# The first tile's queries and keys of each attention, projected into the score banks before the last products of the stage ahead

## What is computed

```python
x = x + band_attention(layernorm(x), ctx, ctx)       # |i - j| <= 128
x = x + ffn(layernorm(x), ...)                        # two layers of:
    h = shift_token(x)                                # half of the columns from the row before
    q, k, v = split(h @ wqkv)                         # 8 heads of 64
    q = l2norm(q) * qs;  k = l2norm(k) * ksc
    q, k = q*cos*scale + rotate_half(q)*sin*scale, k*cos/scale + rotate_half(k)*sin/scale
    x = x + local_attention(q, k, v) @ wo             # back to 256 keys
    h = layernorm(shift_token(x)) * lg + lb
    a, g = split(h @ w1 + b1)
    x = x + (a * gelu(g)) @ w2 + b2
```

## Time and profile before

| | us |
|---|---|
| median of 3 runs | 3050.54 (3049.99 to 3052.98) |
| the profiled execution | 3057.01 |
| its span in the profile | 3055.2 |
| PE busy | 2993.7 (98%) |
| DVE, ACT, POOL busy | 1612.3, 1230.9, 1131.8 |

### The profile page before, as it was taken

How to read it: one execution, slowest core, us unless ns; L and a number is a source line. 1 busy time by engine, 2 the same in 40 slices (tenths; PEclk the granted TensorE clock), 3 DMA queues, 4 the chain that set the end, 5 groups by cost and what they waited for, 6 DMA issues and landing times. The chain is left out here.

```text
span 3055.2 us, 44311 instructions
## 1 busy us (share of the span) xinstructions
PE 2993.7 (98%) x17096; PEld 2437.0 (80%) x17096; DVE 1612.3 (53%) x3359; ACT 1230.9 (40%) x2497; POOL 1131.8 (37%) x1200
## 2 busy tenths in 40 slices
PE   7999999999999999999999999999999999999999
PEld 6787888888878887888877888888878778787777
DVE  5975667766764333333324667766665333333332
ACT  5864555555554111111123555555565211111111
POOL 6755556655641110111103655666551111121111
PEclk8999999999999999999999999999999999999999
DMA  6642111111131111010122111111123111111110
GB/s 232 202 161 78 42 43 46 56 42 53 35 117 46 42 42 42 32 33 20 42 91 61 32 43 53 48 47 39 53 77 110 52 42 35 39 55 52 43 53 26
DMA packets 142582, 187.75 MB, mean 61 GB/s; under 512 B 21094, under 2 KB 74858, under 8 KB 142372
## 3 DMA queue, kind: packets, MB, share of 16 engines
q1 hardware_dynamic: 142372, 184.92, 18.9%
HBM read 132.44 MB, written 52.46 MB: 61 GB/s over the span
## 5 line engine op out<-in xcount | busy, mean ns | idle before, releaser
L938 PE MATMUL quad<-fhT_f,w_h_f 128*128 128x512 f32 (+1 forms) x1392 | 551.1, 396 | 1.5 <-ACT w_h_f L988 1.5
L940 PE MATMUL quad<-fhT_f,w_l_f 128*128 128x512 f32 (+1 forms) x1392 | 545.2, 392 | 0.0
L939 PE MATMUL quad<-fhT_f,w_h_f 128*128 128x512 f32 (+1 forms) x1392 | 543.8, 391 | 0.0
L1559 DVE SCALAR_TENSOR_TENSOR u_f<-quad,bias_f,gate_f 128x512 f32<-128x512 f32 (+1 forms) x174 | 130.2, 749 | 632.1 <-PE quad L940 557.0
L1139 ACT ACTIVATE lprob<-lprob,small 128x384 f32<-128x384 f32 (+2 forms) x512 | 288.6, 565 | 155.7 <-DVE small L1425 155.6
L1713 POOL TENSOR_TENSOR turned_qk<-with_cos,with_sin 128x256 f32<-128x256 f32 x256 | 188.7, 758 | 425.7 <-DVE with_cos L1450 369.2
L720 PE MATMUL bank_pair<-wqkv_h,hT 128*128 128x512 f32 x1024 | 330.8, 404 | 0.5 <-DVE with_sin L1450 0.5
L988 ACT ACTIVATE uT_f<-u_f 128x512 fp32r<-128x512 f32 (+1 forms) x176 | 111.3, 632 | 540.7 <-DVE u_f L1559 532.6
L1235 ACT ACTIVATE gate_f<-quad,bias_f 128x512 f32<-128x512 f32 (+1 forms) x174 | 119.5, 687 | 507.9 <-PE quad L940 507.9
L940 PEld LDWEIGHTS quad<-fhT_f,w_l_f 128*128 128x128 f32 (+1 forms) x1392 | 256.8, 184 | 63.0
L938 PEld LDWEIGHTS quad<-fhT_f,w_h_f 128*128 128x128 f32 (+1 forms) x1392 | 257.1, 185 | 60.8 <-ACT w_h_f L988 2.4
(11 more groups left out here) (201 smaller groups left out, 6108.5 us busy)
## 6 DMA issues: line engine op xcount, KB each, us to landing
s_in<-stream SPq DMA_DIRECT2D x128, 128.0 KB, 2.8
s_res<-stream SPq DMA_DIRECT2D x64, 256.0 KB, 2.8
stream<-a_out SPq DMA_DIRECT2D x64, 256.0 KB, 2.0
res_f<-stream SPq DMA_DIRECT2D x63, 256.0 KB, 3.0
w_h_f_raw<-in_L_ffn_w SPq DMA_DIRECT2D x60, 256.0 KB, 5.3
h_in_f<-stream SPq DMA_DIRECT2D x112, 128.0 KB, 2.3
x_in<-in_x SPq DMA_DIRECT2D x32, 256.0 KB, 2.8
ctx_in<-in_ctx SPq DMA_DIRECT2D x32, 256.0 KB, 3.0
```

The lines of the kernel that those rows point to most:

```text
L938: e.matmul(bank[0:n, :], high, hT[:, 0, c, :], start=c == 0, stop=False)
L939: e.matmul(bank[0:n, :], high, hT[:, 1, c, :], start=False, stop=False)
L940: ins = e.matmul(bank[0:n, :], low, hT[:, 0, c, :], start=False, stop=c == KC - 1)
L1559: e.scalar_tensor_tensor(out=Fm.u[q % 2][0:n, :], in0=up_bank(2 * (g * HC + j) + 1)[0:n, :], scalar=Fm.bias1[0:n, 0, j:j + 1], in1=Fm.gate ...
```

## The change

For tile 0 of each layer Q and K go into `quad[:, 2:4, :]`, and their 24 matmuls stand ahead of the last product of the stage before (`band_mix(31)`, `down(7, 10)`); V of tile 0 comes after it. Tile 0 is squared and rotated in step 0, where it was step 1; tile 1 stays in step 2. In layer 1 the first rows are turned and split one block earlier, behind `down(7, 8)`. The waits of `project` follow the new banks.

```diff
+    def qk_banks(t):
+        return bank_pair if t else quad[:, 2:4, :]
+    def rotated_tile(s):
+        return 0 if s == 0 else s - 1 if 2 <= s <= TILES else None
...
-                bank = banks[0] if part == 2 else bank_pair[:, part, :]
+                bank = banks[0] if part == 2 else qk_banks(t)[:, part, :]
...
+                    elif t > 1:
+                        w.wait_ge(S("with_sin"), 2 * n - 1 + part)
+                    elif t:
+                        w.wait_ge(S("f_out") if l else S("x1") if part else S("total_low"),
+                                  base - 2 + part if l else TILES if part else BATCH)
+                    elif l:
+                        w.wait_ge(S("gate") if part else S("u"), l * GROUPS * HC - 1 + part)
                     else:
-                        w.wait_ge(S("with_sin"), 2 * n - 1 + part)
...
+                        w.wait_ge(S("score_max"), TILES)
...
                 if s == TILES + 3:
-                    project(0, 0, 0, 12)
+                    project(0, 0, 12, 36)
...
+                if s == 0:
+                    turn_h(1)
+                    project(l, 0, 0, 12)
...
+                    if l + 1 < DEPTH and (g, j) == (GROUPS - 1, 9):
+                        turn_first_rows(l + 1)
             if l + 1 < DEPTH:
-                turn_first_rows(l + 1)
+                project(l + 1, 0, 12, 36)
             down(GROUPS - 1, FULL)
...
-                if t == 0:
+                if t == 0 and l:
+                    w.wait_ge(S("down"), GROUP * GROUPS * HC * l)
+                elif t == 0:
                     wait_phase()
...
-                    if d == 0 and 1 <= s <= TILES:
-                        square(s - 1)
+                    if d == 0 and rotated_tile(s) is not None:
+                        square(rotated_tile(s))
+                    if (s, d) == (0, 0):
+                        split_h(l, 1)
...
-            if l + 1 < DEPTH:
-                split_first_rows(l + 1)
+                    if l + 1 < DEPTH and (g, j) == (GROUPS - 1, 9):
+                        split_first_rows(l + 1)
             finish_group(GROUPS - 1)
```

More of the change, by code:

```diff
@@ L787, in scores @@
                     w.wait_ge(S("u") if l else S("score_max"), GROUPS * HC * l if l else TILES)
+                    w.wait_ge(S("with_sin"), 2 * n + 2)
                 w.wait_ge(S("lprobT"), 2 * (U - 1))
@@ L864, in attend @@
                         scores(t, d)
-                    if inside and (l, s, d) > (0, 0, 0):
+                    if inside:
                         project(l, s, PROJECTED[d][0], PROJECTED[d][1])
@@ L1131, in square @@
                     w.wait_ge(S("early_store"), 16 * (l * GROUP + i + 1))
-                e.activation(flat(A.square[:, :, :]), flat(bank_pair), ACT.Square).then_inc(S("squared"), 1)
+                e.activation(flat(A.square[:, :, :]), flat(qk_banks(t)), ACT.Square).then_inc(S("squared"), 1)
             def probabilities(t, h):
@@ L1196, in attend @@
                         keep_v(s)
-                    if d == 0 and s + 1 < TILES:
+                    if d == 0 and 1 <= s < TILES - 1:
                         split_h(l, s + 1)
@@ L1475, in attend @@
                             maximum(t, h)
-                    if d == 0 and 1 <= s <= TILES:
-                        rope(s - 1, 0, A.with_cos, A.rope_cos, "with_cos")
-                        rope(s - 1, 0, A.with_sin, A.rope_sin, "with_sin")
-                        norm_sum(s - 1)
+                    if (s, d) == (0, 0):
+                        split_h(1)
+                    if d == 0 and rotated_tile(s) is not None:
+                        rope(rotated_tile(s), 0, A.with_cos, A.rope_cos, "with_cos")
+                        rope(rotated_tile(s), 0, A.with_sin, A.rope_sin, "with_sin")
+                        norm_sum(rotated_tile(s))
                     if early is not None:
@@ L1492, in attend @@
                             attend_split(l, 3, quarter)
-                    if d == 0 and 1 <= s <= TILES:
-                        rope(s - 1, 1, A.with_cos, A.rope_cos, "with_cos")
-                        rope(s - 1, 1, A.with_sin, A.rope_sin, "with_sin")
-                    if d == 0 and s + 1 < TILES:
+                    if d == 0 and rotated_tile(s) is not None:
+                        rope(rotated_tile(s), 1, A.with_cos, A.rope_cos, "with_cos")
+                        rope(rotated_tile(s), 1, A.with_sin, A.rope_sin, "with_sin")
+                    if d == 0 and 1 <= s < TILES - 1:
                         split_h(s + 1)
```

26 lines of the change are left out of this document (11 added, 15 removed).

## The result

The changed kernel takes 3058.07 us in the median of 10 runs (3055.64 to 3059.73), the kernel before 3051.48 us in 10 runs beside them (3048.70 to 3053.61). The ratio is 1.0019, 95% interval 1.0010 to 1.0028: the change costs some 6 us, between 3 and 8.5. The forecast was +9.0 us and slower. The prediction drew its own line for slower at 0.2%, 6.1 us; by it the result stays undecided, 6.6 us by the medians and 5.8 by the ratio.

What follows compares the result with a forecast made beforehand. PE is 98% busy, so only its waits count; rotation waits for tables behind each stage's last product. Layer 0 2.8 + layer 1 5.0 + clock 1.2 = 9.0 us on 3050.5 gives 3059.5 us, forecast 3057 to 3062 (0.62).

Steps and rivals of the forecast that it cites:

- The gate: Start of both layers: rotation waits for POOL's tables, and these for the stage's last product, not for the squares.
- Layer 0, 2.8 us: Twelve more matmuls ahead of `band_mix(31)` delay tables and rotated keys; layer 0 loses 2.8 us.
- The wait at V of tile 1: A new PE wait of about 3 us ahead of V of tile 1 in both layers.
- Layer 1, 5.0 us: Twenty-four matmuls ahead of `down(7, 10)` cost 5.6 us, 0.6 comes back from an earlier split; layer 1 loses 5.0 us.
- The piece from keys to scores (6.2 us) is untouched: Layer 1: the 6.2 us from rotated keys to scores stay, as the split of `wo` keeps its place.
- The clock, +1.2 us: PE's lower clock behind longer waits: half a slow group of twelve matmuls in layer 0, nothing in layer 1; +1.2 us.
- rival A: The chains slide but slow stretches shorten or vanish: +3.5 us at best, 3054.0 up to 3056.6 us; chance 0.14.
- full clock behind the waits: Sign against the forecast: it is wrong if the granted clock behind the waits is at its full level.
- The slow stretch under V and Q of tile 1: Upper clock bound: tile 1's V and Q run slow in layer 0, PE comes 2.4 us late to the keys.
- C: Rival: rotation begins with the squares, so layer 1's keys and scores come 3.2 us earlier; -6 us, 3044.5; chance 0.04.
- D: Rival: no change, the kernel's later waits absorb the slide; 3050 to 3053 us; chance 0.07.
- B: Rival: the clock falls earlier and stays low; +14.2 us, 3064.7 us; chance 0.13.

Runs made afterwards that it cites:

- e4: The kernel before, with POOL's tables made early in both layers as in e3; 3049.72 us against 3051.66, ratio 0.9995.
- e3: The changed kernel, with POOL making the tables ahead of the last band offset (layer 0) and of `residual(31)` (layer 1); 3053.67 us against 3051.66 for the kernel before.
- e1: The change kept for layer 0 alone, layer 1 as in the kernel before; 3055.41 us against 3051.66 for the kernel before, ratio 1.0011.
- e8: As e6, but only tile 28's part of `down(7, 10)` stands ahead of Q and K, the other three behind; 3049.80 us against 3051.77 for the kernel before.
- e9: As e8, with the load of tile 31's residual queued on SP ahead of the stores of tiles 29 and 30; 3045.45 us against 3051.76 for the kernel before.
- e5: The changed kernel, with the last band product and last down-projection ahead of all projections of tile 0; 3048.40 us against 3051.77 for the kernel before.
- e6: As e5, with POOL making layer 1's tables ahead of `residual(31)`; 3046.15 us against 3051.77 for the kernel before, ratio 0.9983.
- e2: The change kept for layer 1 alone, layer 0 as in the kernel before; 3057.67 us against 3051.66 for the kernel before, ratio 1.0014.

## Why the prediction was right, and where it was off

**The gate.** Right. `with_cos` is released by POOL's tables in both layers of the changed kernel, e4 turns the releaser into the square at almost no gain, and e3 brings two thirds of the loss back by the tables' place alone (by the time; by the traces 2.4 us).

**Layer 0, 2.8 us.** Measured 2.6 us on the keys in e1, and 3.4 us in its time. The wait at V of tile 1 was put at 3 us and is 2.86. The step from there to "Layer 0 loses 2.8 us" was not right: at tile 3 of e1, 1.3 us are left.

**Layer 1, 5.0 us.** The keys are 4.8 us later with the transposes counted, and at tile 3 2.7 us are left. The wait at V of tile 1 was put at some 3 us and is 3.17; the one at the queries was put at 3.5 and is 1.56. "The piece from keys to scores (6.2 us) is untouched" holds in code only: it took 5.7 us in the changed kernel, since PE turned the keys at full clock (0.65 us for 1.11). One step of the chain was read too short. The text has the load of tile 31 wait for tile 28's store; it also waits on SP's queue behind the stores of tiles 29 and 30, as e8 and e9 show. In the changed kernel both end at nearly the same time, so the number was right, but whoever splits the down-projection by the chain as I wrote it gets e8.

**The clock, +1.2 us.** This term was mis-sized and has the wrong sign, and it is the step that put the forecast above the measured time. The chain terms by their keys are 2.6 us (e1) and 4.8 us, together 7.4. At tile 3 the changed kernel has lost 5.6 us. The difference, -1.8 us, is what the clock did in these profiles, since the other waits up to tile 3 are the same within 0.1 us. It has two parts. Under the moved matmuls of layer 0 the lower clock made the chain 1.6 us longer, a place that the prediction did not look at. Behind the keys 3.4 us came back, 1.3 in layer 0 and 2.1 in layer 1, because PE passed the first scores and the projections behind them with less time at the lower clock than in the kernel before. The prediction had put nothing there for layer 1. That is rival A's mechanism, and the sign named in the prediction, full clock behind the waits, is there in layer 0 and not in layer 1. The slow stretch under V and Q of tile 1 that I argued for is there too (in the changed kernel and in e1), but PE still waits 0.74 us for the keys behind it, so it costs nothing there.

How far is one profile to be trusted here? Summing the granted clock over 45 us from the first projection and from the layer 1 reference gives 3.4 and 13.7 us at the lower level in the kernel before, 10.2 and 10.2 in the changed one. But e1 has the code of the kernel before in layer 1 and spends 6.8 us there. Its tile 3 still comes within 0.6 us of the kernel before, as much of that slow time fell into waits. Layer 0 of the changed kernel is the same code in e1, and there tile 3 is 1.6 us apart, for the moved matmuls alone. So two executions of one code differ by up to 1.6 us at tile 3. With e1's layer 0 the clock's part would be -3.4 us and the whole 4.0. The sign holds in both, the size does not.

**The hit.** The median of 3058.07 us lies in the forecast's range from 3057 to 3062, and part of that is luck. The kernel before is at 3051.48 us in ten runs, 0.9 above the three that the forecast stood on; on the old base the same 6.6 us give 3057.1.

**The rivals.** C, that early squares pay, is refuted for this order. In e5, with the last products ahead, the tables are still what `with_cos` of layer 1 waits for, so the early squares win nothing there either. Only with early tables as well do they pay: `with_cos` of layer 1 waits for the square in e4 (16.2 us) and no longer in e6 (13.6), 2.3 us earlier with the transposes counted. No run moves the squares alone. The price that the change pays is not in rotating early but in what it put the projections in front of. D has no support. A and B differ from the forecast by the clock alone; with 6.6 us the measurement lies between A (3.5 to 6.1 us) and the forecast. The Trainium skill's advice in "Perfetto Trace Analysis", section "Optimization Strategy", to let the dependencies of a waiting engine start sooner is borne out by e5 and e6, once it is applied to the dependency that ends last: `residual(31)` and the tables, not the squares.

## What to carry to other kernels

When work is moved ahead of a stage's last product, follow that product's result through every engine and queue to the next thing PE waits for: 24 matmuls of filling work moved the head of a chain of 22 us by 5 us, and PE waited at its end. A set-up operation that stands last on an idle engine out of habit (the tables), or a load that stands behind stores which it does not need (tile 31's), is worth looking for first, since no run here shows a price for moving it. A delay at the first tile is not yet a loss: read it again some tiles on, where the waits have settled. Before pricing the clock from a profile, look at how the same stretch runs in a second one.

## What the runs showed of the hardware

The slow stretches of TensorE need no single long wait ahead of them. The kernel before falls to the lower level at 257 us behind waits of 0.50, 1.06 and 1.82 us, while the longer wait of 2.15 us for tile 0's rows is followed by full speed there and in e1. In the changed kernel the granted clock is 0.62 in 232 to 234 us, behind the same wait and with the same instructions ahead of it as in e1. A stretch of 24 matmuls of 512 columns took 5.6 us in the one case (e1) and 7.2 in the other.

A store's time to land varies as well. Tile 28's store took 2.0 us from issue to landing in the kernel before and in the changed one, and 4.1 us in e2 and e3, with PE's order ahead of it as in the changed kernel.
